# Routed mixture-of-experts stage: row tiles fetched one tile ahead and copied by VectorE, last tile in steps of 64 rows, expert registers loaded early

## What is computed

```python
x = x + attention(layernorm(x))          # 16 heads, decay mask, group norm, Wout
x = x + ffn(layernorm(x))

def ffn(x):                              # per row, 8 experts, 1024 -> 1408 -> 1024
    topk_w, topk_i = top_k(softmax(x @ gate_w.T), 2)      # the 2 best experts
    topk_w = topk_w / sum(topk_w)
    eo[e] = (silu(x @ w_gate[e]) * (x @ w_up[e])) @ w_down[e]
    out = sum_e combine[e] * eo[e]       # a row gets only its 2 experts
    return out + sigmoid(x @ sg) * ((silu(x @ sw_gate) * (x @ sw_up)) @ sw_down)
```

## Time and profile before

| | |
|---|---|
| time, median of 3 runs | 2179.98 us (2174.4 to 2189.42) |
| the profiled execution's own time | 2164.92 us |
| its span, slowest core (core 7) | 2163.4 us |
| other cores' spans | 2120.9 to 2162.1 us |
| TensorE busy, core 7 | 2027.5 us (94%) |
| weight loads on TensorE | 1242.7 us (57%) |
| VectorE, ScalarE, GpSimd busy | 37%, 26%, 10% |
| granted TensorE clock | 0.973 to 0.977 on every core |

### The profile page before, as it was taken

How to read it: one execution, slowest core, us unless ns; L and a number is a source line. 1 busy time by engine, 2 the same in 40 slices (tenths; PEclk the granted TensorE clock), 3 DMA queues, 4 the chain that set the end, 5 groups by cost and what they waited for, 6 DMA issues and landing times. The chain is left out here.

```text
span 2163.4 us, 37870 instructions; the slowest of 8 cores (2120.9 to 2163.4 us)
## 1 busy us (share of the span) xinstructions
PE 2027.5 (94%) x14227; PEld 1242.7 (57%) x14227; DVE 789.7 (37%) x1945; ACT 559.6 (26%) x967; POOL 223.6 (10%) x197
## 2 busy tenths in 40 slices
PE   6999999966979999999969999999999999999997
PEld 3444444432434444444437777777777767767775
DVE  5677777675325544555311111111111111111111
ACT  1333333321212112211202222223223232222222
POOL 1000000000210111011101111111111111111101
PEclk9999999977989999999989999999999999999999
DMA  9733334465773224322497868778677877777533
GB/s 200 135 99 97 98 98 98 117 131 121 132 200 117 89 109 157 117 89 109 124 182 115 132 105 131 118 115 134 114 128 120 134 112 127 131 111 129 94 54 50
DMA packets 260389, 258.35 MB, mean 119 GB/s; under 512 B 194201, under 2 KB 200604, under 8 KB 258082
## 3 DMA queue, kind: packets, MB, share of 16 engines
q0 software_dynamic: 55440, 140.28, 38.2%
q1 hardware_dynamic: 204818, 116.36, 21.8%
HBM read 219.65 MB, written 83.49 MB: 140 GB/s over the span
## 5 line engine op out<-in xcount | busy, mean ns | idle before, releaser
L1364 PE MATMUL ffn_ps<-r_xT,w 128*128 128x256 bf16 (+1 forms) x6688 | 687.3, 265 | 31.4 <-PEq L1198 31.4
L1364 PEld LDWEIGHTS ffn_ps<-r_xT,w 128*128 128x128 bf16 x6688 | 613.1, 98 | 109.8 <-issue 36.4
L1294 DVE TENSOR_TENSOR r_h<-r_si,ffn_ps 128x256 bf16<-128x256 bf16 (+1 forms) x418 | 165.9, 400 | 875.8 <-DVEq L1198 874.1
L1073 PE MATMUL ffn_ps<-xln2T,w 128*128 128x512 bf16 x1408 | 307.0, 380 | 2.5 <-DVE sh_h L1086 2.5
L1274 ACT ACTIVATE r_si<-ffn_ps 128x256 bf16<-128x256 f32 (+1 forms) x418 | 151.8, 367 | 425.5 <-ACTq L1198 422.7
L394 PE MATMUL att_ps<-xlnT,w 128*128 128x512 bf16 x1024 | 237.8, 382 | 1.2 <-DVE xlnT L348 1.1
L1073 PEld LDWEIGHTS ffn_ps<-xln2T,w 128*128 128x128 bf16 x1408 | 136.8, 98 | 166.0 <-issue 4.6
L1322 POOL DMA_INDIRECT out<-r_y,r_meta x70 | 111.0, 1586 | 695.0 <-POOLq L1198 657.9
L1374 PE MATMUL ffn_ps<-w,r_h 128*128 128x512 bf16 x770 | 169.3, 379 | 0.0
L1374 PE MATMUL ffn_ps<-xca,r_h 128*128 128x512 bf16 x770 | 169.3, 379 | 0.0
L394 PEld LDWEIGHTS att_ps<-xlnT,w 128*128 128x128 bf16 x1024 | 96.0, 98 | 116.0 <-issue 4.6
(11 more groups left out here) (152 smaller groups left out, 1121.1 us busy)
## 6 DMA issues: line engine op xcount, KB each, us to landing
xca<-x SPq DMA_DIRECT2D x48, 512.0 KB, 5.7
w<-wu POOLq DMA_DIRECT2D x16, 1408.0 KB, 13.3
w<-wg POOLq DMA_DIRECT2D x8, 2112.0 KB, 15.2
combT_d<-cb SPq DMA_DIRECT2D x8, 1024.0 KB, 4.9
x1b<-x SPq DMA_DIRECT2D x16, 512.0 KB, 5.2
out<-xca SPq DMA_DIRECT2D x16, 512.0 KB, 3.4
out<-x1b SPq DMA_DIRECT2D x16, 512.0 KB, 3.7
xca<-wd POOLq DMA_DIRECT2D x4, 2048.0 KB, 14.4
```

The source lines that it names most:

```text
L1073: i = q.matmul(b_, wslot[w][:, dt * IFF + it * C:dt * IFF + (it + 1) * C], xT2[t % 2][:, dt, :], start=(dt == 0), stop=(dt == 7))
L1294: v.tensor_mul(h[:, it, 0:rt], rsi[:, it % 4, 0:rt], bank(2 + it % 4)[:, RT:RT + rt]).then_inc(r_h, 1)
L1364: i = q.matmul(bank(2 + it % 4)[:, c0:c0 + rt], w_[:, dt * IFF + it * C:dt * IFF + (it + 1) * C], xT[:, dt, 0:rt], start=(dt == 0), stop=( ...
```

## The change

1. The transposed rows land in a new buffer `r_xTn`; VectorE copies it to `r_xT` at the head of each tile and frees `r_xTn` at once, and TensorE waits for the copy (`r_xr`) instead of for the DMA. So a tile's rows are fetched while the tile before is computed.
2. GpSimd copies the row numbers out of the meta into `ids`, uses them for the indirect DMA, and frees the meta before the DMA is done.
3. The routed buffers are laid out anew (`r_skip`), so that ScalarE need not wait for the stores of step 7; VectorE waits for the scatter and clears `r_h` in the last down projection.
4. TensorE and VectorE load all 16 expert registers in the last down projection, two per group of 11 matmuls.
5. The last tile is done in steps of 64: a rest of up to 64 rows as a 64-row tile, up to 128 as 128, up to 192 as 192, above as a full tile. Each engine now has three such tiles behind the loop, each behind a branch (`If_eq(kind, k)`).

```diff
-        tblf = sb3("tblf", [C, 5, 8], F32)
...
+        def load_regs(q, e):
+            full, kind = q.alloc_register("full%d" % e), q.alloc_register("kind%d" % e)
+            q.reg_load(full, tbl[0:1, 3, e:e + 1])
+            q.reg_load(kind, tbl[0:1, 6, e:e + 1])
+            return full, kind
...
                     i.then_inc(p_dn.h, 1)
+                    if t == NTILE - 1:
+                        if g == 0:
+                            wait(q, late["cnt"])
+                        pe_regs.append(load_regs(q, g))
...
+                    if t == NTILE - 1:
+                        if g == 0:
+                            wait(v, late["sct"])
+                            v.memset(late["h"][:, :, :], 0.0)
+                        dve_regs.append(load_regs(v, g))
                     wait(v, done)
...
-    def tile_loop(q, n, full, tile):
+            yield e, regs[e][0], regs[e][1]
+
+    def tile_loop(q, full, kind, tile):
         with q.If_ne(full, 0):
             with q.Fori(0, full, 1):
                 tile(RT)
-        with q.If_ne(n, full):
-            tile(RT // 2)
+        for k in range(1, RT // RS):
+            with q.If_eq(kind, k):
+                tile(k * RS)
...
         wait(a, cnt_tok)
-        wait(a, out_stored[1])
         a.sem_inc(r_yfree, 1)
...
             def tile(rt):
+                take(v, r_xfull, 16)
+                v.tensor_copy(xT[:, :, :], xTn[:, :, :]).then_inc(r_xfree, 1)
+                v.drain().then_inc(r_xr, 1)
                 for it in range(NIT):
...
                 take(g, r_yfull)
+                g.tensor_copy(ids[:, hf:hf + 1], meta_i[:, hf, 0:1])
+                g.drain()
                 g.indirect_dma_start(
...
             def tile(rt):
-                take(q, r_xfull, 16)
+                take(q, r_xr)
...
-                            if hf == 0 and dc == 0 and it == 0:
-                                i.then_inc(r_xfree, 1)
```

More of the change, by code:

```diff
@@ L30 @@
 RT = 256
+RS = 64
 REG = L + RT
@@ L1011, in v2 @@
                 if t_cnt is not None:
-                    n, nt, nf, w = (tblf[:, k, :] for k in range(4))
+                    n, nt, nh, w, nf, kd, sm = (tmp[k // 4][:, k % 4, :] for k in range(7))
+                    v.drain()
                     v.tensor_sub(n, base[:, 4, :], ebase)
@@ L1055, in emit_ffn @@
         h_hist = [None, None]
+        def load_regs(q, e):
[3 more added lines that the diff above has]
+            return full, kind
+        pe_regs, dve_regs, late = [], [], {}
         dn_free = [None] * 4
@@ L1183, in emit_ffn @@
         wout_done = wpe
-    xT = sb2("r_xT", [C, 8, RT], BF16)
+    xTn = sb2("r_xTn", [C, 8, RT], BF16)
     h = sb2("r_h", [C, NIT, RT], BF16)
@@ L1200, in emit_ffn, with expert_tiles @@
     out_stored = [(st[i].h, st[i].n) for i in range(2)]
-    def expert_tiles(q):
-        n, full = q.alloc_register("n_tiles"), q.alloc_register("n_full")
+    def expert_tiles(q, loaded=None):
+        regs = loaded or [load_regs(q, e) for e in range(8)]
         for e in range(8):
-            q.reg_load(n, tbl[0:1, 0, e:e + 1])
-            q.reg_load(full, tbl[0:1, 3, e:e + 1])
-            yield e, n, full
-    def tile_loop(q, n, full, tile):
+            yield e, regs[e][0], regs[e][1]
+    def tile_loop(q, full, kind, tile):
         with q.If_ne(full, 0):
@@ L1267, in act_routed @@
         wait(a, cnt_tok)
-        wait(a, out_stored[1])
         a.sem_inc(r_yfree, 1)
-        for e, n, full in expert_tiles(a):
+        for e, full, kind in expert_tiles(a):
             def tile(rt):
@@ L1277, in tile @@
                 take(a, r_yfree)
-                for hf in range(rt // C):
+                for hf in range((rt + C - 1) // C):
                     for dc in range(2):
@@ L1284, in tile @@
                     a.drain().then_inc(r_yfull, 1)
-            tile_loop(a, n, full, tile)
+            tile_loop(a, full, kind, tile)
     em("scalar", act_routed)
     def dve_routed(v):
-        wait(v, cnt_tok)
-        for e, n, full in expert_tiles(v):
+        for e, full, kind in expert_tiles(v, dve_regs):
             def tile(rt):
+                take(v, r_xfull, 16)
+                v.tensor_copy(xT[:, :, :], xTn[:, :, :]).then_inc(r_xfree, 1)
+                v.drain().then_inc(r_xr, 1)
                 for it in range(NIT):
@@ L1295, in tile @@
                                  bank(2 + it % 4)[:, RT:RT + rt]).then_inc(r_h, 1)
-            tile_loop(v, n, full, tile)
+            tile_loop(v, full, kind, tile)
     em("vector", dve_routed)
@@ L1311, in pool_routed @@
         wait(g, out_stored[1])
+        n = g.alloc_register("n_tiles")
         left = g.alloc_register("left")
         half = g.alloc_register("half")
-        for e, n, full in expert_tiles(g):
+        for e in range(8):
+            g.reg_load(n, tbl[0:1, 0, e:e + 1])
             g.reg_load(half, tbl[0:1, 5, e:e + 1])
@@ L1347, in pe_routed @@
     def pe_routed(q):
-        wait(q, cnt_tok)
         wait(q, v_dn_last)
-        for e, n, full in expert_tiles(q):
+        for e, full, kind in expert_tiles(q, pe_regs):
             sl = 3 * ((e + 1) % 2)
@@ L1377, in tile @@
                                          start=(it == 0), stop=(it == NIT - 1))
-                            if hf == 0 and dc == 0 and it == 0:
-                                i.then_inc(r_xfree, 1)
                         i.then_inc(r_y, 1)
-            tile_loop(q, n, full, tile)
+            tile_loop(q, full, kind, tile)
     em("tensor", pe_routed)
```

48 lines of the change are left out of this document (29 added, 19 removed).

## The result

The changed kernel takes 2242.66 us in the median of four runs (2238.12 to 2248.85) against 2183.18 for the kernel before: ratio 1.029, 95% interval 1.025 to 1.033. It is slower by 2.9%, where the prediction said no measurable change, in a range up to 2210 us. The profiled execution has core 7 at the end, and every core is slower than before, by 59 to 100 us (compare).

The account below looks back on a forecast made before the run. TensorE, busy 94% of the span, was taken as the bound. Stall, gap and last-tile gains against jump costs put core 6 last at 2166.8, 3.4 over 2163.4; added to the 2180 median: 2183 us, 8-in-10 range 2143 to 2210.

Parts of the forecast that it names:

- the first tile: Routed stage's first tile: TensorE's 15.45 us stall, from ScalarE's wait for step 7's stores, goes; 17.3 us won on core 7.
- the register loads: TensorE's expert register loads in the last down projection: 0.7 us per group, hidden by the sequencer's 3.6 us lead, costing nothing.
- J - 2.7 us: Ends of experts: for J us of jumps TensorE starts the next tile this late, plus 1.65 of clock where over 2 us.
- the steps: Core 7's sum: 2163.4 + 44.2 for jumps - 18.2 old gaps - 17.3 first tile - 22.7 last tiles = 2149.4 us.
- GpSimd's copy: GpSimd's copies of the row numbers: off the path but for the last one, under 0.5 us.
- The price of a jump: TensorE's branches over unused last tiles at ends of experts: 4.2 us for a long jump, 0.35 for a short one.
- My counting of blocks: TensorE's program in 256-instruction blocks: jumps reaching the next block are short, those reaching the second next are long.
- The clock: Full tiles behind a gap of over 2 us run at 1.2 GHz for a moment: 1.65 us more each.
- the last tiles: Experts' rests: 64 rows instead of 128 save 3.0 us, 192 instead of 256 save 4.7; 22.7 us on core 7.
- The second rival: Jumps on TensorE: every passed block is a wait of its own, 4.2 us each; time 2201, chance of over 2202 0.25.
- The 1.2 us per passed block: Extra for each whole block a jump passes beyond the earlier long jumps: six on core 6, +7.2 us, at most +25.2.
- the cheap jumps: First rival: later blocks are present, all jumps take 0.35 us; time 2122, or 2136 with one long per boundary; chance 0.22.

Follow-up runs that it names:

- e9: Changed kernel without GpSimd's drain, one 64-row last tile, next transpose issued before the meta wait, ScalarE's wait for step 7's stores put back: ratio 0.989, 0.977 without that wait.
- e1: The changed kernel with GpSimd's drain replaced by a semaphore that its copy raises: span 2208.0 us on core 7; timed again, ratio 1.012 to the kernel before.
- e6: As e1, with one more branch around the three last-tile branches: no ratio given; core 6's span 2126.2 us against 2190.2 in e1.
- e7: As e5, but the one last tile has 64 rows, larger rests being full tiles: median 2137.21 us, ratio 0.981 to the kernel before.
- e5: The changed kernel without GpSimd's drain and with the old single 128-row last tile behind one branch: median 2155.6 us, ratio 0.990 to the kernel before.
- e4: The kernel before with only the last tile changed, to three tiles in steps of 64 behind three branches: median 2216.57 us, ratio 1.020.
- e2: The changed kernel with the old single 128-row last tile behind one branch, drain kept: median 2219.01 us, ratio 1.019 to the kernel before.
- e3: The changed kernel with part 2 undone whole (no row-number copy, no drain, meta freed after the DMAs landed): median 2235.06 us, ratio 1.027.

## Why the prediction was wrong

What held: the first tile (stall gone; e9 shows that the wait was its whole cause); the 64-row tile at about 7 us; no gap at the first copy, and only 0.42 us at the register loads; the branches as what the change adds; the fit that the next tile starts J - 2.7 us late. With core 6's three jumps of 17.5 us behind expert 0 it gives 14.8, measured 14.86; with core 7's of 17.8 behind expert 6, 15.1, measured 15.31.

As a time the miss is 60 us, 2242.66 against 2183; core 7, and not 6 or 1, ended last. What failed, for core 7, where the steps gave -14.0 and the profile shows +80.6, a difference of 94.6 us (more than 60, because the profiled execution before ended 15 us under the median, and because core 7's stage started late in the one after):

- **GpSimd's copy, "off the path but for the last one, under 0.5 us": 35 us** (gaps of 101 with the drain, 66 without; behind one branch instead of three the same drain costs 58, so the share belongs to this order of taking things away). I priced the copy and not the drain in the same two lines, and did not follow what the release of the meta holds up: SyncE's queue is in order, and the next transpose stands in it behind the meta load. The kernel before had a late release too, when the adds had landed, but there the transpose had to wait for TensorE to read the old rows as well, and the gaps behind 128-row tiles stayed at 0.4 to 3.4 us.
- **The price of a jump: 30 us** (gaps of 35.9 without the clock predicted, 66 in e1). Three things. The jumps are dearer than 4.2 us: over the eight cores of the changed kernel the 36 pairs take 9.8 us in the mean and the 28 triples 15.8 (16.6 where all three jumps are long). All 72 jumps of the pairs are long, 3.0 us or more, so the short ones that I gave three pairs by their place (two on core 7, one on core 1) did not come. The one that I gave a triple of core 1 did, 0.36 us behind expert 3. Place does decide there: the first jump of a triple is short behind experts 3 and 7, on each core that has one (5 of 5), and long behind all others (23 of 23). My counting of blocks holds for such a first jump at best. And in e1 TensorE stands another 5 us after the last branch in two places on core 7 (before the 192-row tile and behind expert 4), as in e6 without a branch or a wait.
- **The start of the routed stage: 20.6 us**, in no term of mine; see below.
- **The clock: 4 us, the last tiles: 5.5.** The six full tiles behind the gaps of 12.0 to 19.2 us take 21.0 to 21.8 us (1.6 to 2.4 more, not 1.65); the granted clock was 0.50 in the first 4 us of that behind expert 1. A 64-row tile won 2.4 us, not 3.0, since there are small stops within it (3.9 us in all, "issue"), and the 192-row tile won 2.9, not 4.7; the clock was at 0.50 at its start too, for which the sum had 1.65 of its own.
- The old gap before the first tile shrank by 0.8.

20.6 + 35 + 30 + 4 + 5.5 - 0.8 = 94.3 of the 94.6.

The second rival ended on the right side at 2201, and for the wrong reason: its mechanism, a wait for each passed block, is refuted by e6. The 1.2 us per passed block in my sum should have been 0, the price per jump 4.9 to 5.5. (Where the prediction's paragraph on the skill says "second rival", the cheap jumps are meant, its first.) What no rival had is that the thing that was to hide the fetch of the rows made it later.

**What stays open.** Why the routed stage starts late on cores 6 and 7. Their steps 4 to 6 take 74 to 76 us where others take 72. By line, gate and up of the shared expert from 830 to 1100 us, core 7 and core 1:

```profile
L1086 PE MATMUL ffn_ps<-xln2T,w 128*128 128x512 bf16 x680 | 153.3, 388 | 13.8 <-DVE sh_h L1099 13.8
```

```profile
L1086 PE MATMUL ffn_ps<-xln2T,w 128*128 128x512 bf16 x689 | 149.7, 379 | 1.5 <-DVE sh_h L1099 1.5
```

VectorE waits there for ScalarE's silu, and ScalarE stands up to 4.3 us without a wait, while GpSimd scatters rows. It is hardly the change's work: the program in these steps is that of before, six cores don't show it, and it moves from one pair of cores to another (2 and 3 in e7, start at 1138.6 and 1133.5; 4 and 5 in e5, 1137.7 and 1137.4, and in e4, 1122.9 and 1121.9, a kernel with none of the change but its tail). The kernel before has something like it: in one timed run cores 4 and 5 end at 2154.6 and 2161.2 us, in its profile at 2120.9 and 2130.2. The median of the timed runs is 59.5 us over before, about the routed stage's 60.4 us on core 7. The spans of these runs say that the late start is no fixed part of them: core 6 ends at 2240.7 in the profiled one and at 2204.6, 2225.3 and 2212.7 in the others. What makes one jump dearer than another isn't settled either. Single ones take 3.9 us in the mean in e5 and 5.9 in e2, which differs by the drain alone; the last of three takes 7.1 in e1, the first 4.0, where all three are long. Other traffic on the DMA engines, and a fetch that the jump before has started, would both fit, but no run tests them.

## What to carry to other kernels

Price each instruction that an edit adds, the drain more than the copy before it, and ask what it waits for; then follow the release behind it through every in-order queue, because a buffer that is freed late holds back whatever stands behind its refill. Code that is jumped over costs per taken jump and not per length: put one branch around all variants rather than one behind the other. And when two causes are waited for at the same moment, test them in all four combinations, since undoing one alone hides most of what it costs.

## What the runs showed of the hardware

- A drain on GpSimd lasts until the DMAs that GpSimd issued have landed: 6.3 us in the median, up to 15.0, where the work behind it was a copy of 0.2 to 0.8 us. Where no such DMA is in flight it takes 0.9 us at most. A semaphore raised by the copy orders copy and indirect DMA as well, and the DMA follows 1.0 us after the copy's start.
- A long jump on TensorE takes 3.3 to 5 us when it stands alone, over 411 instructions (e5) or 1,290 (e6) alike (up to 7.3 in e2, with the drain); in pairs and triples it takes 3 to 8.5, about 5 in the mean. A single jump over 411 instructions, or the first of a triple, can also take 0.36 us; in the kernel before, the changed one, e4 and e5 the place of the expert decides which, alike on all cores but behind expert 3 in the kernel before. The same branches on VectorE took under 0.1 us.
- A transpose issued 2.4 us behind a weight load landed after 25.2 us, the same transpose 5.7 us ahead of it in 6.8. Over all such transposes of e3 it took 13.3 to 26.2 us.
